# A context loop whose first block of rows is loaded behind the strip writes and split between the two probability halves

## The reference

```python
Q_char = _linear(char_emb, Wq_c, bq_c)          # 256 latent rows
K_sub = _linear(subword_emb, Wk_s, bk_s)        # 25088 context rows
V_sub = _linear(subword_emb, Wv_s, bv_s)
scores = jnp.einsum('bqh,bkh->bqk', Q_char, K_sub) * scale
char2sub = jnp.einsum('bqk,bkh->bqh', jax.nn.softmax(scores, axis=-1), V_sub)
```

## Time and profile before

| what | value |
|---|---|
| median of 3 runs | 1169.48 us (1167.11 to 1169.86) |
| the profiled execution, its own time | 1165.06 us |
| its span on the core | 1163.3 us |
| PE busy | 1038.4 us, 89% of the span |
| DVE busy | 618.1 us, 53% |
| ACT busy | 372.8 us, 32% |
| DMA | 381.48 MB, mean 328 GB/s |
| the context loop | from about 88 us to about 590 us of the span |

### The profile page before, as it was taken

The page is one execution under the profiler, slowest core; times in us unless marked ns, Lnnn a source line. Parts: engine busy times, 40 slices in busy tenths (PEclk is TensorE's granted clock), DMA queues, the critical chain, the costliest instruction groups (busy, mean ns, idle before and its releaser), DMA issues.

```text
span 1163.3 us, 16777 instructions
## 1 busy us (share of the span) xinstructions
PE 1038.4 (89%) x6736; PEld 714.6 (61%) x6736; DVE 618.1 (53%) x977; ACT 372.8 (32%) x546; POOL 3.5 (0%) x20
## 2 busy tenths in 40 slices
PE   9999999999999999999999999999887666667666
PEld 8867878878888888888866756454432222222223
DVE  4457878878878878878854365222121111111112
ACT  2444456546546556546433252000000000000000
POOL 1000000000000000000000000000000000000000
PEclk9999999999999999999999999999997898997989
DMA  9548799887888887888859435999999999999997
GB/s 347 188 145 301 284 350 349 305 297 282 286 296 284 285 303 278 286 298 282 287 193 384 145 145 230 428 425 425 426 426 426 428 428 428 428 428 429 426 429 308
DMA packets 91122, 381.48 MB, mean 328 GB/s; under 512 B 5584, under 2 KB 6224, under 8 KB 74064
## 3 DMA queue, kind: packets, MB, share of 16 engines
q1 hardware_dynamic: 91088, 381.00, 84.1%
HBM read 355.29 MB, written 25.69 MB: 327 GB/s over the span
## 4 chain that ended last, share of the span: by engine, by line
DMA 47%; PE 27%; DVE 17%; SPq 4%; ACT 2%; issue 2%; DVEq 0%; ACTq 0%
DMA deep<-in_r_down 23%; DMA strips<-turned 11%; DMA pt<-strips 9%; DVE nat_lo L1261 4%; DVE turned L1288 4%; PE ps L984 4%; DVE pt_lo L1266 4%; SPq L351 3%; DMA wide<-in_r_up 3%; DVE st L1273 2%; ACT pt_hi L1052 2%; PE ps L544 2%; PE ps L970 2%; PE ps L964 1%; DMA nat<-in_ctx_rows 1%
## 5 line engine op out<-in xcount | busy, mean ns | idle before, releaser
L558 PE MATMUL ps<-ctt_hi,q_hi 128*128 128x512 f32 x392 | 153.7, 392 | 0.0
L560 PE MATMUL ps<-ctt_hi,q_lo 128*128 128x512 f32 x392 | 152.6, 389 | 0.0
L559 PE MATMUL ps<-ctt_lo,q_hi 128*128 128x512 f32 x392 | 152.5, 389 | 0.0
L571 PE MATMUL ps<-nat_hi,pt_hi 128*128 128x512 f32 x368 | 143.8, 391 | 3.9 <-DVE pt_lo L1266 3.9
L573 PE MATMUL ps<-nat_hi,pt_lo 128*128 128x512 f32 x368 | 143.3, 389 | 0.0
L572 PE MATMUL ps<-nat_lo,pt_hi 128*128 128x512 f32 x368 | 143.3, 389 | 0.0
L1205 ACT ACTIVATE sg<-ps 128x256 f32<-128x256 f32 x32 | 12.3, 384 | 388.0 <-PE ps L964 388.0
L1602 DVE TENSOR_TENSOR hh<-sg,ps 128x256 f32<-128x256 f32 x32 | 13.5, 421 | 227.7 <-PE ps L970 227.7
L984 PE MATMUL ps<-deep,hh_t 128*32 128x512 f32 x496 | 77.9, 756 | 54.9 <-DMA deep<-in_r_down 53.6
L1256 DVE TENSOR_TENSOR ctt_lo<-ctt,ctt_hi 128x2048 fp32r<-128x2048 f32 x49 | 111.0, 2289 | 18.6 <-ACT ctt_hi L1044 18.2
L1048 ACT ACTIVATE nat_hi<-nat 128x2048 fp32r<-128x2048 f32 x48 | 92.1, 1918 | 79.4 <-DMA nat<-in_ctx_rows 79.4
(11 more groups left out here) (281 smaller groups left out, 1257.4 us busy)
## 6 DMA issues: line engine op xcount, KB each, us to landing
wide<-in_r_gate SPq DMA_DIRECT2D x32, 2048.0 KB, 26.0
wide<-in_r_up SPq DMA_DIRECT2D x32, 2048.0 KB, 27.4
deep<-in_r_down SPq DMA_DIRECT2D x31, 2048.0 KB, 25.8
ctt<-in_ctx_t SPq DMA_DIRECT2D x49, 1024.0 KB, 7.9
nat<-in_ctx_rows SPq DMA_DIRECT2D x48, 1024.0 KB, 7.4
strips<-turned SPq DMA_DIRECT2D x96, 256.0 KB, 5.1
pt<-strips SPq DMA_DIRECT2D x24, 1024.0 KB, 4.8
w_gate<-in_w_g_t SPq DMA_DIRECT2D x2, 1024.0 KB, 13.6
```

Source lines behind the costliest of these rows:

```text
L558: mm(o, qh, ctt_hi[par][:, c, :], start=(c == 0), stop=False)
L559: mm(o, qh, ctt_lo[par][:, c, :], start=False, stop=False)
L560: last = mm(o, ql, ctt_hi[par][:, c, :], start=False, stop=(c == HC - 1))
L571: mm(o, p_hi[:, w, :], n_hi[:, t, :], start=(first and t == 0), stop=False)
```

## The change

In SP's program, `spread(u)` is cut in two: `spread(u)` now holds only the wait for `turned` and the four strip writes, and a new function `gather_strips(u)` holds the wait for these and the read into `pt`. In `pair(u)` the strip writes come first, then the wait for the products and the load of `nat[0]`, then the read into `pt`. This holds for pairs 1 to 23; pair 0 keeps its order.

In DVE's `pair(u, par)` the low part of the rows of half 0 (`rows_lo` into `nat_lo[0]`) moves from in front of the first `block_max` to between the two calls of `probs_lo`. This holds for u = 2 to 23, so 22 times. The last stretch behind the loop, written out apart, keeps its order.

```diff
@@ sync, spread @@
             def spread(u):
 
-
                 sp.wait_ge(s["turned_ready"], u * 2 + 2)
                 for g in range(G):
                     sp.dma_start(strips.rearrange("(k j) g n -> j k g n", k=G)[:, :, g, :],
                                  turned[g * Q:(g + 1) * Q, :, :, :, :].rearrange("j k h w i -> j k (h w i)")
                                  ).then_inc(s["strips_stored"], 16)
+
+            def gather_strips(u):
+
                 sp.wait_ge(s["strips_stored"], u * (16 * G) + 16 * G)
                 sp.dma_start(pt[:, :, :, :, :].rearrange("p g h w i -> p (g h w i)"), strips.rearrange("p g n -> p (g n)")
                              ).then_inc(s["pt_loaded"], 16)
@@ sync, pair(u) @@
                 else:
                     load_columns(u * 2 + 3, 1)
+                spread(u)
                 sp.wait_ge(s["products_done"], u * 2 - 1)
                 load_rows(u * 2, nat[0], nat_loaded[0])
-                spread(u)
+                gather_strips(u)
                 sp.wait_ge(s["products_done"], u * 2)
                 load_rows(u * 2 + 1, nat[1], nat_loaded[1])
@@ sync, before the first pair @@
             load_columns(3, 1)
             spread(0)
+            gather_strips(0)
@@ vector, pair(u, par) @@
                 accumulate(u - 2, par)
-                rows_lo(u * 2 - 2, nat[0], nat_hi[0], nat_lo[0])
                 block_max(u * 2, 0)
                 probs_lo(u * 2 - 2, 0)
+                rows_lo(u * 2 - 2, nat[0], nat_hi[0], nat_lo[0])
                 probs_lo(u * 2 - 1, 1)
                 step(block_max(u * 2 + 1, 1))
                 pair_bias(par)
```

## The result

| kernel | median | runs | span of the profiled run |
|---|---|---|---|
| before | 1168.30 us | 1163.46 to 1169.86 (4) | 1163.3 us |
| changed | 1246.92 us | 1243.97 to 1251.46 (4) | 1242.2 us |

The changed kernel takes 1.0688 times as long, with a 95% interval of 1.0656 to 1.0720: 78.6 us slower. The direction was forecast, the size was not: 1203 us, with a range from 1187 to 1226.

The account below looks back on a forecast made before the run. PE was taken as the bound, the ring having about 0.3 us to spare. Terms of +2.20, -0.56 and +0.46 us made the turn 23.55 us; 22 pairs add 33 us to 1169.48, giving 1203 us, range 1187 to 1226.

Parts of the forecast that it names:

- the ring: Loop's chain of waits: maximum, bias, exponentials, turn, strip writes, read, pt_hi, pt_lo, next maximum; 21.45 us before, 23.55 forecast.
- term 1: DVE: nat_lo of half 0, now between the two pt_lo, adds 2.20 us to every turn, 22 times.
- the hole between the strips' bytes and the read: DMA queue before the read is issued: traffic at 8 GB/s in 427.50 to 428.00, room for the moved load.
- Term 2: SP's strips, no longer behind the load of nat[0], take 6.2 us instead of 6.76: -0.56 us.
- the free case: Strips with nothing ahead of them in the queue, as in the first pair: 6.02 us.
- Term 3: SP's read into pt, now behind the load of nat[0], takes 5.2 us instead of 4.74: +0.46 us.
- The bound that I set on the other side: Read into pt with the load of nat[0] fully ahead of it: 7.3 us, against 4.74 at the low end.
- the same sum: One turn: 6.58 + 6.2 + 5.2 + 1.10 + 2.27 + 2.20 = 23.55 us, over 22 pairs, added to 1169.48 us.
- Slower still: ACT is late: Rival: half 0's rows land under 1.92 us before pt, delaying pt_hi; turn 25.5, time 1244 us; chance 0.08.
- ACT's margin of 0.7 us: On ACT, rows land some 2.6 us ahead of pt and nat_hi takes 1.92, so 0.7 us remain.
- The rival that ended faster: Strips run at 410 GB/s with nothing ahead, 3.6 us; turn 21.0, PE's waits vanish, 1164 us; chance 0.05.
- the three signs of being wrong: Strips under 5 us; pt landing within 10 us of the first strip; pt_hi starting right behind nat_hi.

Follow-up runs that it names:

- The quarter load: Changed kernel, but pairs 1 to 23 load and split only the first quarter of half 0's rows (256 KB instead of 1 MB): 1159.94 us, ratio 0.9939.
- the two single moves: Changed kernel with one move taken back: only the move on SP kept, 1237.8 us; only the move on DVE kept, 1210.28 us.

## Why the prediction was right or wrong

*Right: what bounds the kernel.* In a pair such as the one that was read the ring had 0.3 us to spare, PE none (the mean of 22.06 us is above PE's 21.77 by the few pairs with strips of about 9 us); the ring became the bound. The quarter load (PE at 100.00 in 100, 1160 us) and the two single moves agree.

*Right in kind and nearly in size: term 1, the subtraction on DVE.* Forecast 2.20 us a pair; alone it costs 1.93 (ring 23.99 where 24.05 was expected). With 2.20 for it the pieces of that run add up to 23.95; its strips were 0.25 us shorter than before (6.97 against 7.22).

*Wrong, the step that failed: the overlap of the moved load with strips and read (terms 2 and 3).* The prediction let 2.1 of the load's 2.6 us run in the hole between the strips' bytes and the read, at 410 GB/s. The runs show that almost none of it is hidden: 2.46 of 2.60 us are paid, part in the strips and part in the read.

Term 2, the strips: I took one pair with 6.76 us as the base and put 6.2 into the sum, "near the free case". The mean over the pairs was 7.22 before and is 7.07 after, 0.87 us above my figure. The load no longer stands ahead of the strips, but it goes out right behind the fourth one and is under way with it. With the load held back until they had landed they took 5.9 us.

Term 3, the read behind the load: forecast +0.46 us, that is a read of 5.2; it is +1.36, a read of 6.19, 0.99 us above my figure. The bound that I set on the other side (7.3) was the right one, 7.43 when the load is fully ahead. The measured value lies between the two, and it depends on where the rows lie in DRAM: 5.87 us for a well placed block, 6.77 for a badly placed one.

The range went wrong with them: its upper end let the read go to 5.7 us only, though 7.3 was named as the bound. With 6.76 for the strips and 7.3 for the read, the same sum gives a turn of 26.21 us and 1261 us.

*The sum.* With strips and read as measured, and the engines' pieces as they were before, the ring closes: 6.58 + 7.07 + 6.19 + 1.10 + 2.27 + 2.20 = 25.41 us, against 25.39 by the strips' issues. So the method held and terms 2 and 3 did not: 22 x (25.39 - 23.55) = 40 us of the miss, 19 by the strips and 22 by the read. The base of 22.06 was right because it was the mean of all pairs.

*Put at nothing without a reason: the stretch behind the loop.* That nothing there absorbs the loss was right, but the stretch, with its own old order, lost 7.2 us more: 4.7 until PE could begin and 2.5 in PE's first matmuls at the lower clock. With 32.7 + 40.5 + 7.2 - 1.2 = 79.2 us the account closes on the 78.9 us between the spans.

*The rivals.* "Slower still: ACT is late" gave 1244 us, near the measured time, but by another mechanism: in the loop `pt_hi` starts when `pt` lands, 0.5 to 0.8 us after `nat_hi` ends, so ACT's margin of 0.7 us held. Its nearness is chance. Behind the loop the chain does go through ACT's `nat_hi`, but from there to `nat_lo` on DVE and not to `pt_hi`. The rival that ended faster, strips that run at the loads' rate, is refuted by the 5.9 us that they took with nothing beside them. None of the three signs of being wrong appeared; none of them looked for strips or a read slower than forecast.

*Not seen at all.* That the move on SP alone costs 70 us. I priced it by the read and forgot who else waits for the load that is moved: `nat_hi` and `nat_lo` of half 0, 4.2 us of work behind a load that went out 1.5 us ahead of the strips before and goes out 3 us behind their first issue now. In the kernel before, that work ended at 430.22, 8.9 us after the strips' first issue, and between it and `pt_lo` DVE stood idle for 0.30 + 2.13 = 2.4 us. With the move on SP alone it ends 14.7 us after the first issue (427.27 against 412.61), 5.7 us later. That is 3.3 us more than this slack, near the 2.98 us a pair that were measured. I saw the slack for the move on DVE and did not ask what the move on SP takes of it.

## What to carry to other kernels

Find the ring of waits that closes from one turn of the loop to the next and compare its length, as a mean over all turns, with the pace of the busiest engine: here 22 us against 21.8, so that work moved onto it costs nearly its full length in every turn (1.93 us of 2.20). When a load is moved back in a queue, price both what is now behind it and who waits for it; and where one transfer goes beside another, take the case where it is fully ahead into the range, for here 2.46 of its 2.60 us were paid. Look at the copy of the last turn behind a loop, for it can keep the old order.

## What the runs showed of the hardware

Four strip writes of 256 KB, from 32 partitions each, run at 211 GB/s together even on an idle queue, about half of the 410 GB/s that the loads reach.

How long a read and a write to DRAM that overlap in time hinder each other depends here on where they lie: the same 1 MB load from a place 2 MB away made the transfer behind it land 0.9 us later (6.77 against 5.87 us), and moving the other buffer by 2 MB exchanged the slow and the fast pairs. Without the overlap odd and even pairs read alike (7.43 and 7.44 us).

The read cut in halves, with runs of 4 KB instead of 8, makes the load behind it take 0.9 us longer from its issue (8.5 against 7.6 us in the mean) though no byte is added. Whether that is by the shorter runs or by the second DMA is not shown.
